# A two-layer decoder: linear attention rewritten as an unrolled pipeline, router moved into cross attention, expert results scattered by token

## The reference, cut to what matters

```python
x = x + line_attention(norm(x), ...)                 # layer 0: 16 heads, causal, softmax over Pluecker scores
x = x + cross_attention(norm(x), ctx, ...)           # 16 heads of 16, softmax over 375 context rows
x = x + experts_top2(norm(x), Wr, br, W1, b1, W2, b2)
x = x + linear_attention(norm(x), Wq, Wk, Wv, Wg, Wo, lepe_w, lepe_b)   # layer 1
x = x + cross_attention(norm(x), ctx, ...)
x = x + experts_top1(norm(x), ...)

# linear attention, 8 heads of 32, after the rotation of q and k by position
kv = einsum('bshd,bshe->bhde', k, v); ksum = k.sum(1); vsum = v.sum(1)
num = einsum('bshd,bhde->bshe', q, kv) * scale + vsum
den = einsum('bshd,bhd->bsh', q, ksum) * scale + S
o = (num / den + depthwise_conv5(v, lepe_w, lepe_b)) * (x_norm @ Wg.T)
out = o @ Wo.T

# experts: 8 of them, 256 -> 1024 -> 256 with relu
logits = x_norm @ Wr + br              # [16, 112, 8]
# layer 0: the two highest per token, weighted by a softmax over the two
# layer 1: the highest per token, weighted by its probability
```

## Time and profile before

| | us |
|---|---|
| median of 3 executions | 1753.49 (1752.35 to 1757.32) |
| profiled execution, its own time | 1737.61 |
| span of that execution in the trace | 1735.5 |
| PE busy, share of the span | 82% |
| DVE, ACT, POOL busy | 43%, 31%, 24% |
| mean granted clock of TensorE, share of full speed | 0.864 |

### The profile page before, as it was taken

How to read it: one execution, slowest core, us unless ns; L and a number is a source line. 1 busy time by engine, 2 the same in 40 slices (tenths; PEclk the granted TensorE clock), 3 DMA queues, 4 the chain that set the end, 5 groups by cost and what they waited for, 6 DMA issues and landing times. The chain is left out here.

```text
span 1735.5 us, 35382 instructions
## 1 busy us (share of the span) xinstructions
PE 1419.8 (82%) x13764; PEld 1099.0 (63%) x13764; DVE 754.8 (43%) x1813; ACT 540.6 (31%) x1222; POOL 414.6 (24%) x502
## 2 busy tenths in 40 slices
PE   5887689999987499999807666658999998759996
PEld 2555456677765499999605555535776766549994
DVE  4555345555522422222345666644555652132224
ACT  2655134555531122222102111102555553112220
POOL 5665200000001344444351111120000000124443
PEclk8999779999995699999858888756999997659997
DMA  6000011111101499999410000001111110139993
GB/s 205 2 2 2 13 28 29 31 33 33 31 6 43 164 328 325 329 322 329 143 56 1 0 0 0 0 13 24 33 35 29 36 28 6 43 128 336 325 323 118
DMA packets 62474, 170.45 MB, mean 98 GB/s; under 512 B 18715, under 2 KB 43659, under 8 KB 48012
## 3 DMA queue, kind: packets, MB, share of 16 engines
q0 software_dynamic: 21120, 130.53, 21.1%
q1 hardware_dynamic: 41228, 38.14, 8.0%
HBM read 139.37 MB, written 12.85 MB: 88 GB/s over the span
## 5 line engine op out<-in xcount | busy, mean ns | idle before, releaser
L912 DVE TENSOR_REDUCE xa_mx<-xa_ps_s 112x2 f32<-112x750 f32 x256 | 241.0, 941 | 245.5 <-PE xa_ps_s L657 242.1
L663 PEld LDWEIGHTS xa_ps_p<-xa_qT,xa_kT 32*125 32x125 f32 x3072 | 197.0, 188 | 112.9 <-ACT xa_p L836 78.7
L663 PE MATMUL xa_ps_p<-xa_qT,xa_kT 32*125 32x112 f32 x3072 | 239.6, 287 | 31.9 <-DVE xa_mx L912 11.1
L836 ACT ACTIVATE xa_p<-xa_ps_p 125x672 f32<-125x672 f32 x256 | 187.0, 730 | 239.6 <-PE xa_ps_p L663 239.6
L657 PE MATMUL xa_ps_s<-xa_kT,xa_qT 32*112 32x375 f32 x1024 | 244.3, 555 | 11.5 <-DVE xa_mx L912 7.7
L1516 PEld LDWEIGHTS ex_ps_h<-ex_xT,ex_w 128*128 128x128 f32 x1792 | 213.3, 195 | 10.4 <-DMA ex_w<-in_experts0a,ex_now 3.9
L1516 PE MATMUL ex_ps_h<-ex_xT,ex_w 128*128 128x128 f32 x1792 | 213.9, 279 | 6.8 <-DMA ex_w<-in_experts0a,ex_now 3.5
L1527 PE MATMUL ex_ps_y<-ex_w,ex_hT 128*128 128x256 f32 x896 | 202.7, 379 | 0.0
L1527 PEld LDWEIGHTS ex_ps_y<-ex_w,ex_hT 128*128 128x128 f32 x896 | 165.9, 190 | 20.2
L1550 ACT ACTIVATE ex_hT<-ex_ps_h,ex_w 128x128 f32<-128x128 f32 x224 | 70.0, 363 | 274.9 <-PE ex_ps_h L1516 268.7
L1562 DVE TENSOR_SCALAR ex_hT<-ex_ps_h,ex_w 128x128 f32<-128x128 f32 x224 | 68.3, 347 | 173.3 <-PE ex_ps_h L1516 172.1
(11 more groups left out here) (271 smaller groups left out, 2224.2 us busy)
## 6 DMA issues: line engine op xcount, KB each, us to landing
xa_kT<-xa_kU SPq DMA_DIRECT2D x128, 93.8 KB
ys<-ex_y SPq DMA_DIRECT2D x56, 128.0 KB
xa_qT<-xa_qU SPq DMA_DIRECT2D x64, 56.0 KB
xn<-rt_xn SPq DMA_DIRECT2D x8, 448.0 KB
cT<-in_ctxT SPq DMA_DIRECT2D x4, 750.0 KB, 8.3
xa_qT<-xa_nmT SPq DMA_DIRECT2D x128, 1.8 KB
x<-in_x SPq DMA_DIRECT2D x4, 448.0 KB, 5.6
out_x<-x SPq DMA_DIRECT2D x16, 112.0 KB
```

Source lines behind the costliest of these rows:

```text
L663: return pe.matmul(bp[0:CT, i, c * S:(c + 1) * S], kT[r:r + 32, b % RB, n, c * CT:(c + 1) * CT], qT[r:r + 32, b % RB, n, :], start=True, s ...
L836: act.activation(p[slot % 4][:, :, :], bp[0:CT, :, 0:NC3 * S], ACT.Exp).then_inc(exped, 1)
L912: dve.tensor_reduce(mx[:, b % 2, j:j + 2, n], bsc[0:S, :, 0:CL], AX, ALU.max).then_inc(maxed, 1)
```

## The change

1. **Router in cross attention.** Once `finish` has added row t−2 to x, POOL computes its rstd, DVE norms it into `x2` at slot 3 (`second_norm`), PE turns it (`row_turn`, slot 6) and multiplies by the router weights (`logits`, slot 7) in the bank `bk`, ACT copies the turned row, DVE adds the bias (`row_logits`) at slot 0 of the next step, and SP stores the row to `xn`. `keys(t + 2, 0)` now also waits until the logits of row t−2 have been read from `bk`. The loop runs one to two steps longer. The bias of the router is broadcast once, into `brb`, before the first `normed_row`. In steps before the first row's rounds, PE has one idle product in each slot where it had none.
2. **Routing** loses norm, turns, logits and stores; its constants are made once, by POOL in the first cross attention, behind the memsets. The running sum over rows takes 4 steps by doubling where it took 16, that over experts 3 where it took 8. A table `trow` is made as well: for each tile slot the row of `ys` that its token has. POOL fetches the weights of tile 0 (always expert 0) at the start of routing, and those of tile 1 once its expert is known.
3. **Experts**: POOL scatters each tile's y by an indirect DMA to the rows in `trow`, where SP stored it in one block.
4. **Combine**: SP loads whole rows of `ys` in the order of tokens, 4 or 8 DMAs of 448 KB; in layer 0 ACT scales the first part and POOL adds it to x, and DVE does the rest.
5. **Linear attention** is written out row by row. Numerators and denominators come out with tokens on the partitions: the 8 denominators of a token are 8 more columns of the product, each in two parts (`low`, `high`) that are added. The convolution is 10 matmuls per row with diagonal `taps`; x gets its new row in one operation.

```diff
+            def row_turn(b):
+                pe.wait_ge(x2_normed, b + 1)
+                pe.wait_ge(k_copied, min(2 * (b + 5), 2 * NB))
+                reused(pe, lg_set, b)
+                for c in range(2):
+                    last = pe.transpose(bk[:, c * S:(c + 1) * S], x2[:, b % 4, c * P:(c + 1) * P], g.ident[0:S, 0:S])
+                last.then_inc(x2_turned, 1)
+            def logits(b):
+                pe.wait_ge(x2_t, b + 1)
+                for c in range(2):
+                    last = pe.matmul(bk[0:S, 2 * P:2 * P + NE], x2T[:, c, :], g.wr[:, layer, c, :], ...)
...
             def keys(b, m):
                 if m == 0:
                     reused(pe, k_copied, 2 * b)
+                    reused(pe, lg_set, b - 4)
...
+                elif on(sb):
+                    idle_products(bp[:, 0, 0:P], 1)
...
+            dve.wait_ge(br_made, 1)
+            dve.tensor_copy(brb[:, :], bk[0:S, 0:NE]).then_inc(br_set, 1)
...
-            for b in range(NB):
-                if b % 4 == 0:
-                    dve.wait_ge(rstd, b // 2 + 2)
-                layer_norm(dve, g, xn[:, b:b + 1, :], b).then_inc(x_normed, 1)
...
-            for b in range(NB):
-                link(dve.tensor_tensor(cum[:, b + 1, :], cum[:, b, :], tot[:, b, :], ALU.add))
+            for n in range(4):
+                old, new, d = sums[n % 2], sums[1 - n % 2], 1 << n
+                link(dve.tensor_tensor(new[:, NB // 2:, :], old[:, NB // 2:, :], old[:, NB // 2 - d:NB // 2 + NB - d, :], ALU.add))
...
+            def scatter(m, slot):
+                pool.wait_ge(y_copied, m + 1)
+                pool.wait_ge(aimed, m + 1)
+                aim(m + 1, (slot + 1) % NW)
+                pool.indirect_dma_start(y_dram, bass.IndirectOffsetOnAxis(ap=to[:, slot, :], axis=0), y[:, slot % 2, :], None) \
+                    .then_inc(stored[slot % 2], 16)
...
+            for n in range(4):
+                for k in range(top):
+                    rows = y_dram[(1 + k * NB + 4 * n) * S:(5 + k * NB + 4 * n) * S]
+                    sp.dma_start(yg[:, 4 * n:4 * n + 4, k, :], rows.rearrange("(b t) d -> t b d", t=S)).then_inc(y_in[n], 16)
...
+            def convolution(b):
+                pe.wait_ge(vT_copied, b + 1)
+                reused(pe, conv_added, b)
+                for m in range(2):
+                    for n in range(TAPS):
+                        last = pe.matmul(bc[0:S, m * P:(m + 1) * P], vT[:, m, n:n + S], taps[:, m, n, :], ...)
+                last.then_inc(conv_made, 1)
```

More of the change, by code:

```diff
@@ L52 @@
 QUADS = H // 4
+NW = 4
 def expert_tiles(top):
@@ L646, in _ @@
                     spread_k(t + 2, 1)
+                if on(t - 2):
+                    store_row(t - 2)
+            for u in range(4):
+                sp.wait_ge(x2_stored[u], 16 * (NB // 4))
         @block.tensor
@@ L769, in _ @@
             last = NB - 1
-            for t in range(-3, NB + 1):
+            pe.matmul(bk[0:S, 0:NE], g.ones[0:1, 0:S], g.br[0:1, layer, :], start=True, stop=True).then_inc(br_made, 1)
+            for t in range(-3, NB + 2):
                 round_of(t, 0)
@@ new lines, in _ @@
+            pe.wait_ge(taps_set, 2 * (TAPS + 1))
+            for m in range(2):
+                last = pe.matmul(bo[0:S, m * P:(m + 1) * P], g.ones[:, 0:S], taps[:, m, TAPS, :], start=True, stop=True)
+            last.then_inc(lift_made, 1)
+            x_turn(0)
+            for t in range(NB + 2):
+                if on(t):
+                    queries_keys(t)
+                if on(t - 1):
+                    keys_values(t - 1)
+                    q_turn(t - 1)
+                if on(t):
+                    values_gates(t)
+                if on(t - 2):
+                    o_turn(t - 2)
+                if on(t - 1):
+                    convolution(t - 1)
+                    numerators(t - 1)
+                if on(t + 1):
+                    x_turn(t + 1)
+                if on(t):
+                    v_turn(t)
+                if on(t - 2):
+                    if t == 2:
+                        pe.wait_ge(lift_set, 1)
+                    out_product(t - 2)
@@ L1225, in route @@
+def route(nc, g, layer, top, wrow, xrow_tile, trow, ew, w_dram):
     ph = Phase(nc, f"rt{layer}")
@@ L1334, in over_e @@
                 return ap.unsqueeze(2).to_broadcast([S, NB, NE])
-            dve.wait_ge(logits, NB)
-            dve.wait_ge(set_p, 8)
-            link(dve.tensor_copy(lg[:, :, :].rearrange("t b e -> t (b e)"), bl[0:S, 0:BE]))
+            for u in range(2):
+                dve.memset(sums[u][:, 0:NB // 2, :], 0.0)
+                dve.memset(ends[u][:, 0:NE // 2], 0.0)
             link(dve.tensor_reduce(m1[:, :], lg[:, :, :], AX, ALU.max))
@@ L1494, in body @@
                     gather(m + 2, (u + 2) % NW)
-            steps(pool, NTILE, 0, TAIL if TAIL >= 2 else TAIL + NW, NW, body)
+                if not isinstance(m, int) or m > 0:
+                    scatter(m - 1, (u - 1) % NW)
+            last = TAIL if TAIL >= 2 else TAIL + NW
+            for m in range(NW):
+                body(m, m)
+            with pool.Fori(1, (NTILE - last) // NW) as i:
+                for u in range(NW):
+                    body(NW * i + u, u)
+            for m in range(NTILE - last, NTILE):
+                body(m, m % NW)
+            scatter(NTILE - 1, (NTILE - 1) % NW)
+            for u in range(2):
+                pool.wait_ge(stored[u], 16 * ((NTILE - u + 1) // 2))
         @block.tensor
```

744 lines of the change are left out of this document (426 added, 318 removed).

## The result

The changed kernel takes 1591.36 us (median of 4 executions, 1572.03 to 1598.19) against 1755.4 for the kernel before (4 executions): a ratio of 0.903, with a 95% interval from 0.894 to 0.911. The forecast was 1603.3 in a range from 1565 to 1638. The profiled execution took 1593.37, its span is 1591.7; the prediction's sum for it was 1587.4.

What follows compares the result with a forecast made beforehand. PE was taken to bound cross attention and experts, a chain of waits linear attention, with serial seams. Terms summed to −150.2 us, from a median of 1753.5 to 1603.3, range 1565 to 1638.

Steps and rivals of the forecast that it cites:

- Linear attention: Whole stage rewritten row by row: 9.5 us a row with PE full, 163.8 in place of 243.3 us, gain 79.5.
- The sum of 9.2: PE's work in one linear attention row, us: 40 short passes 4.68, 512-column records 3.6, 256-column records 0.9.
- Rival A: Linear attention held by waits or the clock: 11 us a row, +21, total 1624 us; chance 0.22.
- The seams: End of each cross attention to routing's first link: 5.9 us left of 41.6, gain 35.7 in each layer.
- Growth of cross attention: Steady rows: six more PE records 0.7 us a row, new wait of keys 0.6; +16.4 in each layer.
- Rival B: Cross attention grows only +4 in place of 16.4 in both layers, total 1578 us; chance 0.17.
- Starts of cross attention: Before row 0: norm delayed by POOL +1.7 and +5.5, idle products −3 each; together −1.3 and +2.5 us.
- Rival D: Clock comes early in both cross attention ramps: −8 us each, total 1587; chance 0.10.
- Inside routing, first tile: Shorter sums in routing −0.9 and −1.9 us; weights fetched early for the first expert tile −2.8 in each layer.
- Combine: End of experts and combine: −20.7 us in layer 0, bounds −25 and −12; −4.2 in layer 1.
- scatter in place of store +1.2: End of experts 0: POOL's scatter instead of SP's store adds 1.2 us before combine's loads start.
- Rival E: In the experts POOL's scatter queues behind the gathers: tile 12.4 us, +287, total 1890 us; chance 0.02.

Runs made afterwards that it cites:

- e2: Changed kernel with three of the convolution's five taps left out; a linear attention row takes 8.26 us against 9.57.
- e1: Changed kernel with DVE's convolution addition and gating ahead of the rotation in linear attention; ratio 0.901 to the kernel before, row 8.67 us.
- e7: Changed kernel with the router's bias added ahead of slot 0's maximum on DVE; a cross attention row takes 17.17 us against 17.71.
- e5: Changed kernel with SP storing y in tile order instead of POOL's scatter, combine reading wrong rows; combine 0 takes 30.3 us against 34.9.
- e8: Changed kernel without the idle products in the ramp; row 0 of layer 0 comes 69.4 us behind the first scores, 69.5 with them.
- e10: Changed kernel with the linear attention of before; ratio 0.958 to the kernel before, that stage 242.6 us.
- e3: Changed kernel with each cross attention's first norm ahead of the constant copies; ratio 0.906 to the kernel before, norm 0.41 us.
- e9: Changed kernel with combine inside the experts' phase, scatter kept, no border between; ratio 0.901 to the kernel before.
- e4: Changed kernel with only combine's loads issued inside the experts' phase, into the weight buffers; ratio 0.908 to the kernel before.
- e6: Changed kernel with the two router products of a row issued three times; a cross attention row takes 18.50 us, 0.79 more.
- e11: Changed kernel with three idle products for one in the last two steps of each cross attention; ratio 0.905 to the kernel before.

## Why the prediction was right, point by point

The terms of what the change was made for came out well, each within 3 us: linear attention, the two seams, combine 0. That the whole sum came so close (−143.9 against −150.2) is in part luck: growth and ends of cross attention came out 9.9 us better than forecast, the starts 6.9 and the two combines 5.5 worse. The step from this sum to the median rested on the 15.9 us by which the median lay above the profiled execution before; after, the median lies 2.0 below it (1591.4 and 1593.4). This took 17.9 off the forecast and the terms put 6.0 back, which gives the 11.9 between 1603.3 and 1591.4.

- **Linear attention** (−79.5, measured −76.9): the mechanism and the size held. A row takes 9.57 where 9.5 was forecast. PE bounds it (e2). The wait of 0.3 that the prediction put on top is 0.69, for a reason that it had named only for other places: DVE beside POOL (e1). The sum of 9.2 was too high in return: without the wait a row takes 8.67; by 0.109 for 0.117 a record (e2) an estimate gives 0.3 of that to its 40 short records. Of its signs one missed: PE was to be busy over 95% and is at 92%. Rival A (11 us a row, clock at 0.84) fell: the clock is at 1.00.
- **The seams** (−35.7 each, measured −36.8): what was left was priced at 5.9 us and takes 4.8.
- **Growth of cross attention** (+16.4 in each layer): the row grew by 0.85, not 1.3. The wait of 0.6 is 0.54 (e7). The 0.7 for the six records is 0.59 of PE's time, of which about a quarter us fell into time in which PE had been idle, so that 0.31 is left (e7); the prediction had argued against that. In the 12 intervals this gives +5.8 and +7.4, less than 12 × 0.85 because before three rows of layer 0 and two of layer 1 took about 18 us. Rival B had the right direction, with too large a size.
- **The ends of cross attention** (a part of the same term): +16.8 in layer 0 and −7.1 in layer 1. The clock fell to 0.50 in the last row of layer 0 here; in the kernel before it fell in layer 1 (0.66 in 1443 to 1465). That was missing from the sum. Kernels with the same code for these steps took 37.0 to 55.2 us there (e1 to e5, e8 to e10), so it belongs to the execution rather than to the change.
- **Starts of cross attention** (−1.3 and +2.5, measured +0.2 and +7.9): the 5.5 for the norm behind POOL's memsets was right (e3 gives 5.1 back; the norm lasts 3.21 and 4.88, as its sign asked). The 3 us expected from idle products were not there: both ramps stayed long, 69.5 and 72.6 us from first scores to row 0. Rival D (clock early in both ramps) did not come about in this execution, but did in e2, e5, e7, e9 and e10.
- **Inside routing, first tile**: −4.0 and −3.2 against −3.7 and −4.7. PE waits 0.65 for the turned x at the first tile where it waited 3.48 for weights. This was not tried apart, and why layer 1 gave less than forecast is open; the row is the last one below.
- **Combine** (−20.7, measured −20.1; −4.2, measured +0.7): the step that failed is "scatter in place of store +1.2". It costs 4.6 us in layer 0 and 8.0 in layer 1 (e5), by POOL's drain at the border (e4, e9). In layer 0 something else made up for a part of it: the first addition came 12.9 us behind the copy (847.56) where the sum had 10.1, but the 16 rows took 22.0 where it had 24.1. The competition between DVE and POOL was forecast at 3: in the rows beside POOL's additions DVE's take 0.83 to 0.90 in place of 0.40, seven of them, which is 3.1 us. An eighth, at 852.10, took 0.40, and there it was POOL's addition that took 1.01 in place of 0.72.
- **Experts** (0, measured +2.6 and −1.2): tiles are at 7.24 in both. In layer 0 one tile took 9.37; why is open. The rest is the first tile: 9.30 before and 9.76 after in layer 0, 9.98 and 8.79 in layer 1. Rival E (scatter behind the gathers) did not come about.

The lines for that competition, from DVE's timeline in combine 0 of the changed kernel, beside and behind POOL's additions:

```profile
851.39 9.48 POOL L1828 TENSOR_TENSOR x<-x,cb_yg 112x256 f32<-112x256 f32 x12 [0.29 <-ACT cb_yg L1821]
853.22 0.83 DVE L1843 TENSOR_TENSOR x<-x,cb_yg 112x256 f32<-112x256 f32 x1
854.07 0.44 DVE L1836 SCALAR_TENSOR_TENSOR cb_yg<-cb_yg,wtop,cb_ps_b 112x256 f32<-112x256 f32 x1
861.01 0.40 DVE L1843 TENSOR_TENSOR x<-x,cb_yg 112x256 f32<-112x256 f32 x1
```

And PE's first tile of layer 0, against the first line of the earlier trace rows:

```profile
576.08 6.25 PE L1720 MATMUL ex_ps_h<-ex_xT,ew_w 128*128 128x128 f32 x32 [0.65 <-ACT ex_xT L1750]
```

The Trainium skill ("SBUF — State Buffer", section "SBUF: two separate sides") says that one of DVE and GpSimd holds the shared port pair for a whole instruction: DVE in a mode that takes two ports or with two inputs in SBUF, the latter only against a GpSimd operation that reads SBUF. By it the gating and the combine's additions had to be slow, the first norm too if it runs in such a mode, and the operations with an input in PSUM not. The traces agree in all three (1.26 and 0.42, 0.83 and 0.40, 4.88 and 0.41), and in combine's weighing of y (L1836), whose bias lies in PSUM: 0.44 beside POOL's additions and 0.45 behind them. That the norm stood through four memsets in a row, and not through one, the sentence does not tell.

## What to carry to other kernels

When work moves to POOL, look at which DVE operation comes to lie beside it, and who waits for that one: the same operation moved by half a microsecond of order gave 0.9 us a row. Put the last indirect DMA of a phase well ahead of its border, or carry the next phase's first work across that border; its cost is not the transfer but what POOL's queue does behind it. A sum made from rows predicts a stage well; what two executions of the same code differ by, here the clock in ramps and tails, has to be known before a change of 1% is judged by whole times.

## What the runs showed of the hardware that was not expected

- A drain of POOL's queue behind an indirect DMA ended 5.8 us (layer 0) and 9.2 us (layer 1) after that DMA's issue in the changed kernel, 3.3 and 6.8 us after its data had been signalled. It lasted the same 3.17 and 6.60 us in all ten traces that keep the scatter and the border (the changed kernel, e1 to e4, e6 to e8, e10, e11); why the layers differ is open.
- DVE's norm stood 4.88 us through four memsets of POOL in a row; in combine DVE's additions and POOL's slowed each other by turns (0.83 in place of 0.40, 1.01 in place of 0.72).
- A matmul record of 8 columns cost 0.10 us of PE's time, one of 128 columns 0.109 (e6, e2).
- The granted clock was 0.50 over 500 to 536 in cross attention 0, with PE busy 35 of 36 us at that clock; the same code kept it up in other executions (e3, e5, e8, e9: 37 to 39 us for rows 12 to 15).
